# A six-layer graph network on one core: VectorE's layer-0 normalise moved one slot on, GpSimd's last-layer shift moved behind layer 0's result

## What is computed

```python
def layer(x, adj):                       # x (128, 128, 256), adj (128, 128, 128)
    q, k, v = x @ Wq + bq, x @ Wk + bk, x @ Wv
    attn = softmax(where(adj == 0, -inf, q @ k.T * scale))
    y = x + (attn @ v) @ Wo
    return (y - mean(y)) * rsqrt(var(y) + EPS) * gamma + beta
```

## Time and profile before

| | |
|---|---|
| time, median of 3 runs | 2490.63 us (2487.67 to 2492.85) |
| the profiled execution | 2490.31 us, of which the trace's span is 2488.5 us |
| TensorE busy (matmul / weight load) | 2363.7 us (95%) / 2179.7 us (88%) |
| GpSimd, VectorE, ScalarE busy | 1843.6 us (74%), 1695.1 us (68%), 1576.8 us (63%) |
| mean granted TensorE clock | 0.990 of full speed |
| chain that ended last | TensorE 65%, VectorE 19%, ScalarE 7%, GpSimd 6%, issue 3% |

### The profile page before, as it was taken

The page is one execution under the profiler, slowest core; times in us unless marked ns, Lnnn a source line. Parts: engine busy times, 40 slices in busy tenths (PEclk is TensorE's granted clock), DMA queues, the critical chain, the costliest instruction groups (busy, mean ns, idle before and its releaser), DMA issues.

```text
span 2488.5 us, 57766 instructions
## 1 busy us (share of the span) xinstructions
PE 2363.7 (95%) x21200; PEld 2179.7 (88%) x21200; DVE 1695.1 (68%) x4945; ACT 1576.8 (63%) x5515; POOL 1843.6 (74%) x2437
## 2 busy tenths in 40 slices
PE   6899999999999999999999999999999999999985
PEld 5789989989989989989889889889889889889874
DVE  4576676676776776776776776776776766766763
ACT  5576666666666666666666666666666666666642
POOL 4577777777777777777777777777777777777763
PEclk9999999999999999999999999999999999999997
DMA  3000000000000000000000000000000000000000
GB/s 145 22 25 31 19 29 31 18 29 31 18 29 27 22 29 27 21 31 27 21 31 25 22 31 22 25 31 23 25 31 23 25 31 22 25 31 12 14 9 13
DMA packets 38728, 68.66 MB, mean 28 GB/s; under 512 B 4400, under 2 KB 12848, under 8 KB 37936
## 3 DMA queue, kind: packets, MB, share of 16 engines
q1 hardware_dynamic: 38448, 64.97, 7.6%
HBM read 48.18 MB, written 16.78 MB: 26 GB/s over the span
## 4 chain that ended last, share of the span: by engine, by line
PE 65%; DVE 19%; ACT 7%; POOL 6%; issue 3%; DVEq 0%; DMA 0%; POOLq 0%; SPq 0%
PE value_bank L406 13%; PE qk_bank L398 12%; PE context_bank L559 8%; PE unit_bank L398 7%; PE qk_bank L512 5%; DVE y L868 5%; DVE y L849 4%; PE unit_bank L469 4%; POOL rstd L961 4%; ACT probs L639 4%; PE unit_bank L406 4%; DVE bn L857 3%; PE score_bank L543 3%; PE unit_bank L481 3%; PE score_bank L540 2%
## 5 line engine op out<-in xcount | busy, mean ns | idle before, releaser
L979 POOL TENSOR_TENSOR x<-y,rows 128x512 f32<-128x512 f32 x320 | 409.5, 1280 | 220.2 <-DVE y L868 218.6
L868 DVE TENSOR_SCALAR y<-y,mv,rstd 128x256 f32<-128x256 f32 x768 | 371.8, 526 | 280.9 <-POOL rstd L961 280.9
L661 ACT CAST xT_hi<-qk_bank 128x512 fp32r<-128x512 f32 x320 | 187.7, 587 | 432.1 <-PE qk_bank L512 432.1
L398 PE MATMUL qk_bank<-xT_hi,w_lo 128*128 128x256 f32 x1280 | 405.4, 317 | 53.5 <-DVE xT_lo L812 53.3
L985 POOL TENSOR_TENSOR x<-x,rows 128x512 f32<-128x512 f32 x320 | 413.4, 1292 | 25.1
L406 PE MATMUL value_bank<-w_lo,xT_hi 128*128 128x256 f32 x1280 | 393.9, 308 | 0.2 <-ACT v L679 0.2
L639 ACT ACTIVATE probs<-unit_bank,negmax 128x128 f32<-128x128 f32 x1024 | 365.5, 382 | 34.8 <-DVE negmax L779 34.8
L398 PE MATMUL qk_bank<-xT_lo,w_hi 128*128 128x256 f32 x1280 | 363.4, 284 | 0.0
L406 PE MATMUL value_bank<-w_hi,xT_lo 128*128 128x256 f32 x1280 | 361.7, 283 | 0.0
L398 PE MATMUL qk_bank<-xT_hi,w_hi 128*128 128x256 f32 x1280 | 361.2, 282 | 0.0
L406 PE MATMUL value_bank<-w_hi,xT_hi 128*128 128x256 f32 x1280 | 360.1, 281 | 0.0
(11 more groups left out here) (93 smaller groups left out, 6477.4 us busy)
## 6 DMA issues: line engine op xcount, KB each, us to landing
x0T<-xT_in SPq DMA_DIRECT2D x64, 256.0 KB, 3.0
x<-x_in SPq DMA_DIRECT2D x64, 256.0 KB, 3.0
out<-x_out SPq DMA_DIRECT2D x64, 256.0 KB, 2.2
adj<-adj_in SPq DMA_DIRECT2D x64, 128.0 KB, 2.1
late_weights<-w_in SPq DMA_DIRECT2D x2, 1024.0 KB, 7.4
rows<-rows_in SPq DMA_DIRECT2D x1, 1792.0 KB, 12.1
probs0T<-w_in SPq DMA_DIRECT2D x4, 256.0 KB, 3.9
x<-w_in SPq DMA_DIRECT2D x1, 1024.0 KB, 13.0
```

The source lines that it names most:

```text
L398: mm = pe.matmul(psum[:, n * G * N:(n + 1) * G * N], split(w, name, kd, at, at + P), flat(xT_half[:, kd]), start=kd == 0 and w is w_lo, st ...
L868: m = dve.tensor_scalar(y[:, r, g], y[:, r, g], mv[:, r, g, 0:1], rstd[:, r, g:g + 1], ALU.subtract, ALU.mult)
L979: pool.tensor_tensor(result(norm), y[:, NORM_AT[norm] % YS], row_of_each(f"gamma{layer}"), ALU.mult).then_inc(zg_ready, 1)
```

## The change

VectorE's `normalise(("group", group))` leaves the end of slot 3 and stands in slot 4 behind `row_max(i - 1)` and `split_lo(i)`. On GpSimd, `shift` of the last layer's item moves behind `scale` and `shift` of the group, so in slot 3 the order becomes `scale` of the item, `find_rstd`, `scale` and `shift` of the group, `shift` of the item. Results are now finished in another order in slot 3, so waits on `x_ready` count with a second table, `RESULT_AT`. No instruction is added or removed.

```diff
+RESULTS = [n for i in SLOTS for n in ([("group", due(i, 2))] if due(i, 2) is not None else []) +
+           ([("item", i - 2)] if item(i - 2) else [])]
+RESULT_AT = {n: at for at, n in enumerate(RESULTS)}
...
-                sp.wait_ge(x_ready, NORM_AT["item", PERIOD * group + STEP * (LAYERS - 2)] + 1)
+                sp.wait_ge(x_ready, RESULT_AT["item", PERIOD * group + STEP * (LAYERS - 2)] + 1)
...
-                pe.wait_ge(x_ready, NORM_AT[source_of(i)] + 1)
+                pe.wait_ge(x_ready, RESULT_AT[source_of(i)] + 1)
...
                 if item(i):
                     split_lo(i)
+                if (group := due(i, 1)) is not None:
+                    normalise(("group", group))
                 if (group := due(i, 2)) is not None:
                     split_headsT(group)
...
                     statistics(("group", group))
-                    normalise(("group", group))
...
                     find_rstd(("group", group))
+                    scale(("group", group))
+                    shift(("group", group))
                 if item(i - 2):
                     shift(("item", i - 2))
-                if (group := due(i, 2)) is not None:
-                    scale(("group", group))
-                    shift(("group", group))
```

## The result

The changed kernel takes 2458.83 us (median of 4 runs, 2457.43 to 2459.18) against 2491.61 us (median of 4 runs of the kernel before): a ratio of 0.987, 95% interval 0.9853 to 0.9887. Forecast were 2459 us and a gain in each period; the size was right, and so was most of the path to it. That the time lies within 0.2 us of the number given is luck: the forecast gain is 31.0 us and the measured one 32.8, and the forecast started from 2490.3 us, 1.3 under the median that it is now compared with.

What follows compares the result with a forecast made beforehand. TensorE, busy 95% of the span, was taken as the bound, stalled in slot 4 of each period. 59 x 0.48 = 28.3 plus 2.7 at the ends gives 31.0 us off 2490.3: 2459 us, range 2438 to 2486.

Steps and rivals of the forecast that it cites:

- gain per period: Per steady period, 59 in all: 0.48 us left of the 1.2 us won in slot 4.
- start and end of the kernel: Outside the steady periods: 1 us gained ahead of them, between 0 and 2, and 1.7 us in the last group.
- The stall removed: Slot 4: the wait on `xT_lo` goes, projection 1.03 us earlier; `kT` wait 0.2 us less; transposes 1.2 us early.
- the bounds 0.74 and 1.67: Join's normalise in its new place: 0.74 us without a GpSimd pass beside it, at most 1.67; 0.74 taken.
- What is given back: Slot 0: about 0.5 us lost ahead of the projection, the rest at the values, leaving 0.48 of 1.2 us.
- The step on GpSimd's queue: Slot 4's `find_rstd` queues behind the shift of `x_out`, starting only 0.29 us earlier while TensorE is 1.2 us earlier.
- Nothing or little is left: Rival: the change moves the stall and no more, 2478 to 2495 us; chance 0.15.
- the eight handovers: Path from normalise through GpSimd's passes to exponentials; half a microsecond more in all together would eat the 0.48.
- More is kept: Rival: slot 4's gain stays whole, 59 x 1.24 + 3 = 76 us, down to 2414 us; chance 0.11.
- Slower: Rival: the join's normalise takes 1.67 us in its new place too, each period 0.45 longer, 2514 us; chance 0.08.

Runs made afterwards that it cites:

- VectorE's part alone: Kernel before, with only the join's normalise moved behind slot 4's row minima and low half, GpSimd's order kept: 2442.06 us, ratio 0.9801.
- GpSimd's part alone: Changed kernel with VectorE's order of before, the join's normalise at the end of slot 3: 2460.79 us, ratio 0.9877.
- the kernel with the late shift: Changed kernel with the shift of `x_out` three slots later, in slot 1, except the last group's: 2421.26 us, ratio 0.9719.

## Why the prediction was right

Point by point, with the changed kernel's times moved by 15.66 us, so that its join add (1200.58) lies on the old one (1216.24):

| step | forecast | measured |
|---|---|---|
| row minima of slot 4 start | 1218.16 | 1218.16 |
| join's normalise, start and length | 1219.12, 0.74 | 1219.12, 0.73 |
| shift of `x_out` starts | 1222.54 | 1222.54 |
| `find_rstd` of slot 4 starts | 1223.78 | 1223.79 |
| row minima of slot 0 start | 1225.48 | 1225.48 |
| projection of slot 4 starts | 1220.75 | 1220.80 |
| transposes at the end of slot 4 | 1223.5 | 1223.60 |
| values of slot 0 start | 1228.67 | 1228.66 |
| gain per period | 0.48 | 0.50 |
| start and end of the kernel | 1 and 1.7 | 1.7 and 1.7 |

*The stall removed.* It was 1.0 us and not the 0.63 in brackets, as read from the starts. The projection came 0.98 us earlier and not 1.03, and `kT` brought 0.16 and not 0.2 (1.14 in all at the transposes, 1224.74 to 1223.60). The key copy stayed last there, as read above. That was without consequence, because the transposes are not what ends last ahead of slot 0's row minima.

*The normalise.* Of the bounds 0.74 and 1.67 the lower held. VectorE's part alone shows why: 1.67 in the new place with the neighbour, and GpSimd's part alone 0.73 in the old place without it. These two settle what in the old trace was one number for two causes. The rule of the Trainium skill's page "SBUF — State Buffer" ("Who interferes with whom") agrees with both rows, as far as the block goes. Whether this instruction is in the two-port mode that the rule names no row shows: alone, one of them takes 0.41 us, as long as the row minima of the same size (0.42), while the mask's `tensor_scalar` of the same size takes 0.29 on average in the changed kernel.

*What is given back.* The step on GpSimd's queue was right, and it is shown and not only argued: the pass doubled costs 1.36 us a period, halved it returns 0.51, out of the way 0.63. Ahead of slot 0's projection 0.44 us were given back and not about 0.5, at the values 0.25, close to the rest that the working left for them.

*What the prediction did not see.* It took the change as one piece. VectorE's part alone would have been 17 us faster than both together, since GpSimd's new order shortens the normalise by 0.94 us and puts a pass of 1.27 in front of `find_rstd` (1.25 from its start to the start of `find_rstd`): 0.31 on balance, against 0.30 measured. All rows for this sum were there. A slip without weight: the next load in SyncE's queue behind the store of slot 3, that of slot 2, is four slots on and not three. At the ends of the kernel 1 + 1.7 were forecast and 1.7 + 1.7 came; the first of them was an estimate between 0 and 2, and no experiment isolates it.

*The rivals.* "Nothing or little is left" needed half a microsecond more in the eight handovers; by the table the chain reached slot 0's row minima at 1225.48, as worked out. "More is kept" needed the shift out of the queue, and so it came, 2421 against 2414 named, when it was moved. "Slower" needed the long normalise behind the new GpSimd order; it never came up, for that order is what makes it short.

## What to carry to other kernels

When an engine's order is changed, redo the timeline of all engines from the old trace, with the handovers as measured, until the moved path meets an instruction that was already last for another reason: the gain is what is left there. Put a pass that nobody waits for where its engine stands idle in the trace, not merely behind the urgent ones, because the next urgent instruction queues behind it. And price the two halves of a change apart: here each alone removed the same stall, and one of them had a cost of its own.

## What the runs showed of the hardware

VectorE's normalise (`tensor_scalar`, 128x256 in fp32, two of them) takes 0.73 us alone and 1.67 beside a GpSimd pass that was started 0.07 us before it, in both places where it was tried. Not every VectorE instruction is held: the row minima at 1225.96 in the earlier trace rows start 0.03 us behind this GpSimd pass and take the same 0.42 us as elsewhere.

```profile
...
1225.93 1.28 POOL L979 TENSOR_TENSOR x<-y,rows 128x512 f32<-128x512 f32 x1 [0.69 <-DVE y L868]
...
```
A very small one is held up as well: `valid` (128x2) takes 0.158 us on average in the changed kernel and 0.842 on average in the kernel with the late shift. In the row shown there it takes 0.94, from 1201.75 to 1202.69, 0.03 us after the end of the shift (1201.38 + 1.28). I had not expected that of two elements per partition. It cost nothing, since VectorE's next row minima still waited 0.62 us for the scores.
